# Forward substitution of the delta rule, its four groups at one block, in four row and column groups of TensorE

## What is computed

```
inv = -(kb @ k.T) * strict_lower            # per chunk, kb = k * beta
for i in range(1, chunk):                   # forward substitution inside a chunk
    inv[i] += inv[i] @ inv
inv = inv + eye
u = inv @ v;  w = inv @ kb
for each chunk: u2 = u - w @ S;  o = q @ S + (q @ k.T * lower) @ u2;  S = S + k.T @ u2
```

## Time and profile before

| | before |
|---|---|
| time, median of 3 runs | 513.18 us (513.15 to 513.31) |
| profiled execution, span | 510.6 us |
| PE busy | 401.5 us (79%) |
| DVE busy | 323.2 us (63%) |
| ACT busy | 159.2 us (31%) |
| chain that ended last | PE 49%, DVE 31%, issue 9%, DMA 5% |

### The profile page before, as it was taken

How to read it: one execution, slowest core, us unless ns; L and a number is a source line. 1 busy time by engine, 2 the same in 40 slices (tenths; PEclk the granted TensorE clock), 3 DMA queues, 4 the chain that set the end, 5 groups by cost and what they waited for, 6 DMA issues and landing times.

```text
span 510.6 us, 8321 instructions
## 1 busy us (share of the span) xinstructions
PE 401.5 (79%) x2952; PEld 293.4 (57%) x2952; DVE 323.2 (63%) x1050; ACT 159.2 (31%) x267; POOL 39.3 (8%) x77
## 2 busy tenths in 40 slices
PE   1979999788973699984245689897998979887992
PEld 0647677467962699971023355565656546564672
DVE  2043464677999823368763576676897588777635
ACT  1252523512345211142021124422433244413430
POOL 7000000002980000000000000000000000000000
PEclk9989999997997555575555969999899989999997
DMA  7460201039653900000000000000020000000000
GB/s 246 105 186 1 42 0 22 1 75 296 166 145 88 119 3 3 3 2 0 1 1 27 15 21 1 0 22 0 2 62 2 21 0 21 0 0 1 22 2 21
DMA packets 48305, 22.23 MB, mean 44 GB/s; under 512 B 17768, under 2 KB 47632, under 8 KB 48016
## 3 DMA queue, kind: packets, MB, share of 16 engines
q1 hardware_dynamic: 31760, 13.40, 10.9%
q10 hardware_dynamic: 16512, 8.39, 6.0%
HBM read 18.64 MB, written 3.15 MB: 43 GB/s over the span
## 4 chain that ended last, share of the span: by engine, by line
PE 49%; DVE 31%; issue 9%; DMA 5%; ACT 3%; SPq 2%; DVEq 0%; ACTq 0%; POOL 0%
PE bank L460 9%; PE bank L493 5%; PE bank L691 5%; PE bank L699 5%; PE bank L721 5%; PE bank L733 4%; PE bank L442 4%; DVE prod L1430 3%; DVE inv L1432 3%; DVE as_t L1410 2%; DVE as_t L1232 2%; DVE nt L1143 2%; DVE nt L1142 2%; DVE as_t L1223 2%; DVE sm L1144 2%
## 5 line engine op out<-in xcount | busy, mean ns | idle before, releaser
L699 PEld LDWEIGHTS bank<-w_sb,as_t 128*128 128x128 f32 x512 | 61.0, 194 | 23.0 <-issue 18.8
L699 PE MATMUL bank<-w_sb,as_t 128*128 128x128 f32 x512 | 63.9, 280 | 5.0 <-ACT as_t L1002 5.0
L1002 ACT ACTIVATE as_t<-bank,cb 128x512 f32<-128x512 f32 x64 | 43.4, 687 | 76.0 <-PE bank L691 60.8
L691 PE MATMUL bank<-as_t,w_sb 128*128 128x512 f32 x128 | 66.5, 648 | 0.0
L1410 DVE SCALAR_TENSOR_TENSOR as_t<-bank,as_t 128x128 f32<-128x128 f32 x128 | 36.0, 344 | 23.4 <-PE bank L699 21.1
L460 PE MATMUL bank<-wtap,xc_pad 128*128 128x384 f32 x128 | 47.0, 514 | 3.8 <-DVE wtap L1157 3.8
L721 PE MATMUL bank<-vb,early 32*32 32x32 f32 x512 | 29.9, 236 | 11.7 <-DMA early<-inverses 11.7
L442 PE MATMUL bank<-ident,as_t 128*128 128x128 f32 (+1 forms) x64 | 12.1, 319 | 33.8 <-DVE as_t L1232 15.7
L1201 DVE TENSOR_TENSOR as_t<-bank,masks 128x512 f32 (+1 forms) x32 | 21.3, 690 | 26.7 <-PE bank L493 26.7
L460 PEld LDWEIGHTS bank<-wtap,xc_pad 128*128 128x128 f32 x128 | 25.0, 202 | 20.3 <-issue 4.3
L721 PEld LDWEIGHTS bank<-vb,early 32*32 32x32 f32 x512 | 28.2, 151 | 13.1 <-issue 12.3
(11 more groups left out here) (221 smaller groups left out, 647.5 us busy)
## 6 DMA issues: line engine op xcount, KB each, us to landing
toep<-taps_long ACTq DMA_DIRECT2D x8, 1024.0 KB, 7.0
toep<-x SPq DMA_DIRECT2D x8, 256.0 KB, 2.8
early<-x SPq DMA_DIRECT2D x4, 256.0 KB, 4.6
w_sb<-w SPq DMA_DIRECT2D x1, 1024.0 KB
w_sb<-w SPq DMA_DIRECT2D x2, 512.0 KB
blocks<-as_t SPq DMA_DIRECT2D x16, 64.0 KB, 2.0
early<-blocks SPq DMA_DIRECT2D x1, 1024.0 KB, 4.9
toep<-ctx_in SPq DMA_DIRECT2D x4, 256.0 KB, 3.4
```

Of the source, the lines that this page charges most:

```text
L691: pe.matmul(ps[4 + half][:, :], w1_sb[:, e, half * 128:half * 128 + 128], x2_c.rearrange("p b t -> p (b t)"), start=True, stop=True).then_ ...
L699: last = pe.matmul(bank(6 + e % 2)[:, b, :], hid[:, e % 2, half, b * L:(b + 1) * L], w2_sb[:, e, half, :], start=(half == 0), stop=(half = ...
L1002: act.activation(hid[:, e % 2, half, :], ps[4 + half][:, :], ACT.Relu, bias=c_of("b1", 2 * e + half)).then_inc(s["hid_ready"], 1)
```

## The change

The four groups are solved together, one block at a time, in two halves of heads (pairs 0 to 7 and 8 to 15 of each group). For this a group has to stand on its own partitions. `inv_t` now has block n of group g on partitions 32g to 32g + 31; it is loaded by 16 DMAs, blocks in order, after both stores have landed. The scaled values are copied by 16 new DMAs from `vb` to the same layout in `vs`, which is the place of `src[:, :, 2, :]`, free once the long filter's last product is done. TensorE takes the pairs with the groups innermost: group g's operands are row group g, its output goes to column group g (first half) or g + 1 (second half) of bank 6, 7, 0 or 1. The applied parts go to column group g of bank 4 or 5. ScalarE copies each group's half (32 of 32 x 256), VectorE subtracts a half of all groups in one operation (6 of 128 x 256). The output products of the first halves of groups 0 and 1 are issued ahead.

```diff
-        inv_t = early[:, 0:NP * CH].rearrange("p (r i) -> p r i", r=NP)
+        inv_t = early[:, 0:NP * CH].rearrange("p (n r i) -> p n r i", n=NC, r=GP)
+        vs = src[:, :, 2, :].rearrange("p (n a) c -> p n a c", n=NC)
...
             sp.wait_ge(s["fir_ps"], CHUNKS)
+            for g in range(NG):
+                for n in range(NC):
+                    sp.dma_start(vs[CH * g:CH * g + CH, n, :, :],
+                                 vb[CH * n:CH * n + CH, GP * g:GP * g + GP, :].rearrange("p (a b) d -> p a (b d)", a=4)
+                                 ).then_inc(vs_in, 16)
...
-            for half in range(2):
-                sp.wait_ge(inverse_out[half], 16)
-                pairs = slice(half * NP // 2, (half + 1) * NP // 2)
-                for n in range(NC):
-                    sp.dma_start(inv_t[CH * n:CH * n + CH, pairs, :], inverse_dram[pairs, n].rearrange("r j i -> j r i")
-                                 ).then_inc(inverse_in[half], 16)
+            sp.wait_ge(inverse_out[0], 16)
+            sp.wait_ge(inverse_out[1], 16)
+            for n in range(NC):
+                for g in range(NG):
+                    sp.dma_start(inv_t[CH * g:CH * g + CH, n, :, :],
+                                 inverse_dram[GP * g:GP * g + GP, n].rearrange("r j i -> j r i")
+                                 ).then_inc(inverse_in[n], 16)
...
+            HALF_R = GP // 2
+            SOLVE_BANKS = (6, 7, 0, 1)
+            def apply_solved(n, half):
+                pe.wait_ge(s["u_ready"], (n - 1) * 2 * NG + (half + 1) * NG)
+                if n >= 2:
+                    pe.wait_ge(s["r_ready"], (n - 2) * 2 + half + 1)
+                for r in range(half * HALF_R, (half + 1) * HALF_R):
+                    for g in range(NG):
+                        last = pe.matmul(ps[4 + half][CH * g:CH * g + CH, r * DH:(r + 1) * DH],
+                                         as_t[0:CH * n, GP * g + r, 0, CH * n:CH * n + CH],
+                                         u[0:CH * n, GP * g + r, :], start=True, stop=True)
+                last.then_inc(s["a_ps"], 1)
+            def solve_blocks(n, half):
+                if n:
+                    pe.wait_ge(s["r_ready"], (n - 1) * 2 + half + 1)
+                for r in range(half * HALF_R, (half + 1) * HALF_R):
+                    for g in range(NG):
+                        c = (g + half) % NG
+                        last = pe.matmul(ps[SOLVE_BANKS[g]][CH * c:CH * c + CH, r * DH:(r + 1) * DH],
+                                         inv_t[CH * g:CH * g + CH, n, r, :], vs[CH * g:CH * g + CH, n, r // H, r % H * DH:(r % H + 1) * DH],
+                                         start=True, stop=True)
+                last.then_inc(s["d_ps"], 1)
+            pe.wait_ge(vs_in, 16 * NG * NC)
+            pe.wait_ge(s["xac_ready"], 1)
+            for n in range(NC):
+                if n:
+                    apply_solved(n, 0)
+                    apply_solved(n, 1)
+                pe.wait_ge(inverse_in[n], 16 * NG)
+                solve_blocks(n, 0)
+                solve_blocks(n, 1)
...
+            pe.wait_ge(s["r_ready"], (NC - 1) * 2)
+            delta_products(0, 0)
+            delta_products(1, 0)
             for g in range(NG + 1):
+                if g < 2:
+                    delta_products(g, 1)
+                elif g < NG:
+                    pe.wait_ge(s["oc_ready"], g - 1)
+                    delta_products(g, 0)
+                    delta_products(g, 1)
...
+                for half in range(2):
+                    act.wait_ge(s["d_ps"], 2 * n + half + 1)
+                    for g in range(NG):
+                        c = (g + half) % NG
+                        first = GP * g + half * GP // 2
+                        act.activation(u[rows, first:first + GP // 2, :],
+                                       ps[(6, 7, 0, 1)[g]][CH * c:CH * c + CH, half * 256:half * 256 + 256
+                                                           ].rearrange("p (r d) -> p r d", d=DH), ACT.Copy
+                                       ).then_inc(s["u_ready"], 1)
...
             for n in range(1, NC):
+                for half in range(2):
+                    dve.wait_ge(s["a_ps"], (n - 1) * 2 + half + 1)
+                    rest = vs[:, n, 2 * half:2 * half + 2, :]
+                    dve.tensor_tensor(out=rest, in0=rest,
+                                      in1=ps[4 + half][:, half * 256:half * 256 + 256
+                                                       ].rearrange("p (a c) -> p a c", a=2),
                                       op=ALU.subtract).then_inc(s["r_ready"], 1)
+                if n < NC - 1:
+                    source_sums(1, B // 2 + (n - 1) * G, B // 2 + n * G, 3)
```

More of the change, by code:

```diff
@@ L217, in decoder_kernel @@
         inverse_out = [sem("inverse_out0"), sem("inverse_out1")]
-        inverse_in = [sem("inverse_in0"), sem("inverse_in1")]
+        inverse_in = [sem(f"inverse_in{n}") for n in range(NC)]
+        vs_in = sem("vs_in")
         xa_in = sem("xa_in")
@@ L712, in _ @@
             pe.wait_ge(s["short_ready"], NG)
[L714 to L722, removed]
-                last.then_inc(s["d_ps"], 1)
@@ L725, in apply_solved @@
[L725 to L747, removed]
-            for g in range(NG + 1):
[L750 to L759, removed]
+            HALF_R = GP // 2
@@ new lines, in _, with delta_products @@
+            pe.wait_ge(vs_in, 16 * NG * NC)
[7 more added lines that the diff above has]
+                solve_blocks(n, 1)
+            def delta_products(g, half):
+                pe.wait_ge(s["u_ready"], (NC - 1) * 2 * NG + (half + 1) * NG)
+                for r in range(half * HALF_R, (half + 1) * HALF_R):
+                    last = pe.matmul(ps[4 + g % 2][r % H * DH:r % H * DH + DH, r // H * L:(r // H + 1) * L],
+                                     u[:, GP * g + r, :], as_t[:, GP * g + r, 1, :], start=True, stop=True)
+                if half:
+                    last.then_inc(s["o_ps"], 1)
@@ L760, in _ @@
+            pe.wait_ge(s["r_ready"], (NC - 1) * 2)
+            delta_products(0, 0)
+            delta_products(1, 0)
+            for g in range(NG + 1):
+                if g < 2:
[4 more added lines that the diff above has]
+                    delta_products(g, 1)
                 if g:
                     pe.wait_ge(s["oc_ready"], g)
-                    if g < 3:
-                        pe.wait_ge(s["u_ready"], NC * NG)
-                    else:
+                    if g >= 3:
@@ L1442, in _ @@
             for n in range(1, NC):
[L1443 to L1447, removed]
-                                      in1=ps[4 + ((n - 1) * NG + g) % 2][rows, :].rearrange("p (r d) -> p r d", r=GP),
+                for half in range(2):
[4 more added lines that the diff above has]
+                                                       ].rearrange("p (a c) -> p a c", a=2),
                                       op=ALU.subtract).then_inc(s["r_ready"], 1)
-                    if g == 1 and n > 1:
-                        source_sums(1, B // 2 + (n - 2) * G, B // 2 + (n - 1) * G, 3)
+                if n < NC - 1:
+                    source_sums(1, B // 2 + (n - 1) * G, B // 2 + n * G, 3)
             dve.sem_inc(s["sums_ready"], 1)
```

## The result

The changed kernel takes **495.21 us** (median of four runs, 494.8 to 496.4) against 513.16 (513.07 to 513.31) for the kernel before in the same session: a ratio of **0.966, 95% interval [0.964, 0.967]**. It is faster, as forecast, but 9 us slower than the 486.2 us forecast; even its shortest run lies 2.8 us above the upper end of the range, 492.0.

The account below looks back on a forecast made before the run. TensorE's matmul passes in the forward substitution were taken as the bound: 29.2 us gained, less 1.2 for clock and 1.0 for gaps, leaves 27.0; span 483.6 plus 2.6 gives 486.2 us, range 481.3 to 492.

Parts of the forecast that it names:

- the price of a pass: Forward substitution on TensorE: 53/4 = 13.3 ns per pass at half clock, so 0.85 us per half of 64 passes.
- no-overlap: Rival: tiles don't overlap when row and column both change; all passes at 53 ns, some 512.3 us; chance 0.04.
- drain: Rival: a change of group drains the array between calls, 0.11 us x 448 = 49 us, giving 562; chance 0.05.
- the copies: ScalarE's 32 copies of 32x256 in the solve: 375 ns each by the line, 1.55 us for the four of a half.
- the subtractions: VectorE's six subtractions of 128x256 in the solve: 0.43 us each.
- the chain within a block: Inverse half 0, latency, copies of both halves, wake-up and apply half 1: 5.12 us from block to block.
- for gaps between issue and pass in a stream four times as dense I book 1.0: Allowance of 1.0 us, set against the 29.2 us gained at the first output transposes.
- two blocks of 5.12 bring block 3: Forward substitution: from block 1's start at 177.6 us, two blocks of 5.12 us put block 3 at 187.8.
- The issue rival: Rival: issue of passes becomes the bound at 26.6 ns a pass, first transposes at 198.8, 488 to 492 us; chance 0.31.
- At 0.49 that is 7.9 us: The sixteen new value copies on SyncE's queue: 0.49 us an issue, 7.9 us together, ahead of x and context.
- covered, with 0.8 us to spare; an issue over 0.54 us begins to cost: ScalarE's square, delayed by the value copies, ends at 171.3 us, before its first copy is due at 172.1.
- 1.2 us in the output tail: Last two groups' output products and transposes if the clock stays at half: 0 to 3 us more, 1.2 booked.

Follow-up runs that it names:

- x3: Changed kernel with each half of passes a two-turn loop over half its pairs, the other pairs left out: 493.56 us (one run).
- x4: Changed kernel with eight unread GpSimd memsets ahead of the copy the first group's output statistics wait for: 492.24 us, ratio 0.958.
- x7: Changed kernel with 32 unread 32x32 calls on TensorE ahead of the first context transposes: 489.09 us (one run).
- x2: Changed kernel with x and context loaded first, block 0's loads for two groups after the first store, VectorE's large sum after block 1's subtractions: 496.08 us, ratio 0.964.
- x5: Changed kernel with sixteen unread GpSimd memsets ahead of the copy the first group's output statistics wait for: 496.64 us.
- x9: Changed kernel with x and context loaded first, 18 unread matmul calls in TensorE's waits and eight unread GpSimd memsets: 488.86 us, ratio 0.956.

## Why the prediction was wrong

**Right: the price of a pass.** 13.3 ns at half clock with four row and column groups; the no-overlap and the drain rivals are dead. Right too, or nearly, were the copies (375 ns, four in 1.57 us against 1.55 booked), the subtractions (0.42 us), and the chain within a block, as x3 shows once supply is relieved (5.64 us from block 2 to 3, 5.12 forecast).

**Wrong, the main step: "for gaps between issue and pass in a stream four times as dense I book 1.0".** They are 6.1 us. The step "two blocks of 5.12 bring block 3" turned into 7.14 and 7.36, 4.3 us more, and from block 3's first pass to the first transposes 7.1 instead of 6.2. The step priced a pass by how fast the array takes it and asked nowhere how fast the instructions arrive. The issue rival came nearer in time (first transposes at 198.8, measured 202.77), and that is luck: its 26.6 ns a pass are close to the 28 at which instructions arrive, but its mark was even starts at 25 ns or more, and the starts are at 13.3 with full stops between. The Trainium skill, "TensorE: Matmul & The Clock Gate", "Wait — 56ns, not 53.3ns?", stood for it with starts never closer than about 25 ns; this trace differs, 13.3 ns over 64 passes. The Trainium skill, "Runtime: NRT & Kernel Launch", "Instruction fetch mechanics", has the blocks of 256 instructions, and the trace agrees (127 or 128 passes from stop to stop). The same section of the Trainium skill calls the cost of crossing a block mostly hidden; here it is 6.1 us of the 29.0 of the stage.

**Wrong, second: the start.** "At 0.49 that is 7.9 us" was 10.4, taken from the median of stores to device memory; "covered, with 0.8 us to spare; an issue over 0.54 us begins to cost" named the point, and it was passed. Block 1 began at 181.13, not 177.6: 3.5 us. Some two of them belong to this execution: its copies begin at 149.45 us, those of x4 and x7, unchanged ahead of the stage but for x7's unread passes, at 147.62 and 147.28, and their blocks 1 begin at 178.95 and 178.90. That leaves some 1.3 us for the queue. In x2 block 1 began where it was forecast, and supply took back 1.1 of the 3.4 us won.

**Wrong, third: the later part was taken to be as long as before** but for 1.2 us in the output tail. The tail ran at full clock (202.77 to 211.8), and that price wasn't due; but the later part grew by 4.4 us: a lead that had risen from 20.4 to 23.7 us lost 8.1 at two long falls of the clock 150 us on.

So: 3.5 + 4.3 + 0.9 = 8.7 us for the first transposes (202.77 against 194.0), 4.4 for the later part, less the 2.2 booked for clock and gaps: 10.9, and 27.0 - 10.9 = 16.1 of the 16.0 that the profiles show. What stays open is why the same instructions settle into long falls in one execution and short ones in another: a wait of 1.60 us for VectorE stands ahead of each long one in the change, but it doesn't decide. In x5 (1.61 us, at 357.88) and x9 (1.61, at 352.69) the same wait stands ahead of falls of 3.4 us, and the long fall of x2 comes without it.

## What to carry to other kernels

When passes get denser, price their instructions too: here 256 instructions of TensorE arrived per 3.6 us, so straight-line code that asks for less than 28 ns a pass for more than a block waits for its program. A loop took 3.1 us off the stage (x3); fewer and wider passes might too, which no run tried. Read "issue" gaps by counting instructions between them, and test them by putting unread instructions ahead. Before booking that a later part stays as it was, look at its granted clock: the same later instructions took 286.0 us in x7 and 291.8 in the change. Filling TensorE's waits with unread matmuls was worth more than it cost: 4.2 us of the later part before the change, 4.0 after it.

## What the runs showed of the hardware that was not expected

- In the dense stage TensorE stops every 127 or 128 passes (256 instructions); transfer 0.9 to 1.3 us, started 1.0 to 1.2 us after the last resumption, passes on 1.4 to 1.5 us after its end.
- Passes of 32x32 over four row and column groups start 13.3 ns apart at half clock, over 64 passes, as the prediction booked without a row for it.
- SyncE's copies of 64 KB from one on-chip buffer to another took 0.60 us an issue, steadily (600/602/739 ns), where stores of the same size had a median of 494.
- VectorE too stopped without a wait in x2, for 3.34 and 1.99 us, each time until 1.3 to 1.5 us after a transfer of instructions.
- 18 unread matmul calls in TensorE's waits shortened the later part by 4.2 us in the kernel before and 4.0 in the changed one, with less half clock behind them.
